# First product of a graph layer on one core: x in five pieces, and the row part of the first four steps on GpSimd

## The reference, cut to what matters

```python
h = maximum(layernorm(x), 0)
a = (adj + adj.T) * 0.5 + eye            # symmetrised, with self loops
deg = sum(a, axis=1)
d = where(deg > 0, deg ** -0.5, 0)
a = d[:, None] * a * d[None, :]
x = x + (adj @ a) @ h                    # first layer
h = maximum(layernorm(x), 0)
x = x + attention_and_dense(h, adj, ...) # second layer: 8 heads, then four dense layers
```

## Time and profile before

| | |
|---|---|
| median of 3 runs | 884.76 us (884.63 to 884.87) |
| profiled execution, time | 884.79 us |
| profiled execution, span | 882.9 us |
| TensorE busy | 855.8 us, 97% of the span |
| VectorE busy | 691.6 us, 78% |
| ScalarE busy | 414.5 us, 47% |
| GpSimd busy | 276.5 us, 31% |

### The profile page before, as it was taken

One profiled execution on the slowest core, in us unless ns is written; L12 is line 12 of the kernel. 1 busy time (PEld: TensorE's weight loads), 2 busy tenths in 40 slices (PEclk: granted clock), 3 DMA queues, 4 the chain that ended last, 5 costly groups with the idle time before them and its releaser, 6 DMA issues.

```text
span 882.9 us, 15244 instructions
## 1 busy us (share of the span) xinstructions
PE 855.8 (97%) x5145; PEld 751.5 (85%) x5145; DVE 691.6 (78%) x1188; ACT 414.5 (47%) x758; POOL 276.5 (31%) x293
## 2 busy tenths in 40 slices
PE   2999999999999999999799999999999999999998
PEld 1878888888888888878699999999999999999663
DVE  6789986556557775686999989999999999999722
ACT  3445433321111122345576666666666666775431
POOL 0000000000000000066738555555555655575222
PEclk9999999999999999999799999999999999999999
DMA  9959922603332321040160000000000032001033
GB/s 349 407 218 373 367 95 77 185 0 119 97 99 90 107 99 54 22 171 4 27 219 16 20 24 26 26 24 24 25 26 24 24 96 72 14 1 49 28 120 140
DMA packets 36117, 87.37 MB, mean 99 GB/s; under 512 B 7072, under 2 KB 7968, under 8 KB 36064
## 3 DMA queue, kind: packets, MB, share of 16 engines
q1 hardware_dynamic: 35024, 82.46, 26.7%
q0 software_dynamic: 1040, 4.26, 1.3%
HBM read 73.93 MB, written 12.78 MB: 98 GB/s over the span
## 4 chain that ended last, share of the span: by engine, by line
PE 90%; DVE 8%; DMA 1%; ACT 1%; issue 0%; ACTq 0%; DVEq 0%
PE bank L1578 25%; PE bank L73 15%; PE bank L75 15%; PE bank L74 15%; PE bank L1604 13%; DVE l_q L1227 3%; PE bank L2036 3%; PE bank L1998 1%; DVE e L859 1%; PE bank L2019 1%; PE bank L2028 1%; DMA l_h<-x 1%; DVE l_stats L784 1%; DVE x_lo L855 1%; PE bank L923 0%
## 5 line engine op out<-in xcount | busy, mean ns | idle before, releaser
L1227 DVE SCALAR_TENSOR_TENSOR l_q<-bank,neg_d,mask 128x512 fp32r<-128x512 f32 x512 | 338.7, 742 | 24.4 <-PE bank L1578 24.1
L1578 PE MATMUL bank<-l_parts,l_q 128*128 128x260 f32 x2048 | 252.0, 284 | 3.8 <-DVE l_q L1227 3.8
L1578 PEld LDWEIGHTS bank<-l_parts,l_q 128*128 128x128 f32 x2048 | 249.3, 190 | 4.3 <-issue 3.9
L73 PE MATMUL bank<-x_hi,s_hi 128*128 128x512 f32 x448 | 174.5, 389 | 0.0
L75 PE MATMUL bank<-x_hi,s_lo 128*128 128x512 f32 x448 | 174.3, 389 | 0.0
L74 PE MATMUL bank<-x_lo,s_hi 128*128 128x512 f32 x448 | 174.3, 389 | 0.0
L746 POOL TENSOR_TENSOR l_prod<-wh,l_a 128x512 f32<-128x512 f32 x30 | 36.3, 1229 | 389.0 <-ACT wh L718 389.0
L1351 ACT ACTIVATE l_mask<-mask 128x512 fp32r<-128x512 uint8 (+1 forms) x256 | 136.4, 619 | 0.1
L1604 PE MATMUL bank<-l_parts,l_mask 128*128 128x260 f32 x1024 | 128.8, 286 | 0.7 <-DVE l_parts L1233 0.7
L1604 PEld LDWEIGHTS bank<-l_parts,l_mask 128*128 128x128 f32 x1024 | 127.0, 189 | 1.0 <-ACT l_o_q L1357 0.9
L75 PEld LDWEIGHTS bank<-x_hi,s_lo 128*128 128x128 f32 x448 | 84.1, 188 | 17.6
(11 more groups left out here) (180 smaller groups left out, 1086.1 us busy)
## 6 DMA issues: line engine op xcount, KB each, us to landing
rows<-adj_t SPq DMA_DIRECT2D x48, 512.0 KB, 3.9
l_now<-adj SPq DMA_DIRECT2D x16, 512.0 KB, 7.5
l_rows_k<-adj_t SPq DMA_DIRECT2D x16, 512.0 KB, 8.3
l_src<-e_rows SPq DMA_DIRECT2D x30, 256.0 KB, 3.2
l_kept<-adj SPq DMA_DIRECT2D x12, 512.0 KB, 13.2
wh_store<-wh POOLq DMA_DIRECT2D x1, 4160.0 KB, 15.8
l_h<-x SPq DMA_DIRECT2D x4, 1024.0 KB, 17.4
x<-x SPq DMA_DIRECT2D x1, 4096.0 KB, 13.5
```

The source lines that it names most:

```text
L73: pe.matmul(acc, hi, rhs_hi, start=first, stop=False, skip_group_check=True)
L1227: v.scalar_tensor_tensor(out=q[:, i, :], in0=bank[S_BANKS[hh]][:], scalar=neg_d[:, i, h:h + 1], in1=mask[:, i, cols], op0=ALU.is_ge, op1=A ...
L1578: return pe.matmul(bank[Q_BANKS[hh][t]][:, 0:PW], q[:, i, t * P:(t + 1) * P], parts[pair_slot][:, hh, i, :], start=i == 0, stop=i == T - 1)
```

## The change

- x is loaded and normalised in five pieces instead of four: tile 0 alone, tiles 1 to 3, and then as before. The load of tile 0's row pieces stands between the first and the second piece.
- The lo part of the row half in steps 0 to 3 is made by GpSimd, in a loop of four subtractions, and counted on a semaphore of its own, early_lo_ready. TensorE in steps 0 to 3, and SyncE's loads of row tiles 4 to 7, wait for that count instead of lo_ready. VectorE adds 4 to lo_ready once.
- VectorE's list is written out for row tiles 0 and 1: the statistics of tile 1 stand between scale(0) and cut_x_lo(0), those of tiles 2 and 3 and the variances behind it; the six refine operations of tiles 1 to 3 are threaded between the small operations of row tile 1.
- ScalarE normalises tile 1 inside step 1 and tiles 2 and 3 one step ahead of their use; tile 0 alone comes first.
- Elsewhere, at the kernel's end, the semaphore last_stored is dropped; the last four stores are counted on the semaphore of their buffer.

```diff
-    CHUNKS = ((0, 4), (4, 8), (8, 12), (12, 16))
+    CHUNKS = ((0, 1), (1, 4), (4, 8), (8, 12), (12, 16))
...
-                sp.wait_ge(lo_ready, (before if before < EARLY else before + EARLY) + 1)
+                if before < EARLY:
+                    sp.wait_ge(early_lo_ready, before + 1)
+                else:
+                    sp.wait_ge(lo_ready, before + EARLY + 1)
...
         load_x(0)
-        for i in range(EARLY + 2):
+        load(0)
+        load_x(1)
+        for i in range(1, EARLY + 2):
             load(i)
-        load_x(1)
+        load_x(2)
...
-        for i in range(EARLY):
+        v.sem_inc(lo_ready, EARLY)
...
+        for i in range(2, EARLY):
             add_now(i)
             add_kept(i)
...
             scale(i)
-            cut_lo(i)
             cut_x_lo(i)
...
+            if i == 1:
+                normalise(1, 1, 2)
             cut_x_hi(i)
+            if i + 1 < EARLY:
+                normalise(1, i + 1, i + 2)
...
+        for s in range(EARLY):
+            p.wait_ge(hi_ready, s + 1)
+            p.tensor_tensor(s_lo[:, s % 2, :], step_source(s), s_hi[:, s % 2, :].bitcast(F32),
+                            ALU.subtract).then_inc(early_lo_ready, 1)
...
-            pe.wait_ge(lo_ready, s + 1)
+            if isinstance(s, int) and s < EARLY:
+                pe.wait_ge(early_lo_ready, s + 1)
+            else:
+                pe.wait_ge(lo_ready, s + 1)
...
-            done.then_inc(self.last_stored if step == 1 else self.stored[c % 2], 16)
+            done.then_inc(self.stored[c % 2], 16)
```

More of the change, by code:

```diff
@@ L153, in smooth_features @@
     lo_ready = sem("l0_lo_ready")
+    early_lo_ready = sem("l0_early_lo_ready")
     x_hi_ready = sem("l0_x_hi_ready")
@@ L202, in sync @@
         load_x(0)
-        for i in range(EARLY + 2):
+        load(0)
+        load_x(1)
+        for i in range(1, EARLY + 2):
             load(i)
-        load_x(1)
+        load_x(2)
         load(EARLY + 2)
         load(EARLY + 3)
-        load_x(2)
         load_x(3)
+        load_x(4)
         for i in range(FIRST_NOW, T):
@@ L219, in link, with statistics @@
             links[name] = len(links) + 1
-        def statistics(c):
+        def statistics(c, skip=0, stop=None):
             lo, hi = CHUNKS[c]
             v.wait_ge(x_loaded[c], 16)
-            for t in range(lo, hi):
+            for t in range(lo + skip, hi if stop is None else lo + stop):
                 v.bn_stats(stats[:, t - lo, :], h[:, t, :]).then_inc(ln_chain, 1)
@@ L309, in vector @@
             refine(0, n)
-        for i in range(EARLY):
+        v.sem_inc(lo_ready, EARLY)
+        add_now(0)
+        add_kept(0)
+        degree(0)
+        guard(0)
+        invert(0)
+        square(0)
+        correct(0)
+        scale(0)
+        statistics(1, 0, 1)
+        cut_x_lo(0)
+        statistics(1, 1)
+        variances(1)
+        add_now(1)
+        refine(1, 0)
+        add_kept(1)
+        refine(1, 1)
+        degree(1)
+        refine(1, 2)
+        guard(1)
+        refine(1, 3)
+        invert(1)
+        refine(1, 4)
+        square(1)
+        refine(1, 5)
+        correct(1)
+        scale(1)
+        cut_x_lo(1)
+        for i in range(2, EARLY):
             add_now(i)
@@ L324, in vector @@
         degree(4)
-        statistics(1)
+        statistics(2)
         guard(4)
-        variances(1)
+        variances(2)
         cut_lo(5)
@@ L330, in vector @@
         invert(4)
-        refine(1, 0)
+        refine(2, 0)
         add_kept(5)
         square(4)
-        refine(1, 1)
+        refine(2, 1)
         degree(5)
         correct(4)
-        refine(1, 2)
+        refine(2, 2)
         guard(5)
         scale(4)
-        refine(1, 3)
+        refine(2, 3)
         cut_lo(6)
-        refine(1, 4)
+        refine(2, 4)
         add_now(6)
-        refine(1, 5)
+        refine(2, 5)
         invert(5)
@@ L362, in vector @@
         cut_x_lo(8)
-        statistics(2)
+        statistics(3)
         invert(7)
-        variances(2)
+        variances(3)
         square(7)
@@ L370, in vector @@
         scale(7)
-        refine(2, 0)
-        statistics(3)
-        refine(2, 1)
+        refine(3, 0)
+        statistics(4)
+        refine(3, 1)
         cut_lo(10)
-        refine(2, 2)
+        refine(3, 2)
         cut_x_lo(10)
-        refine(2, 3)
-        variances(3)
-        refine(2, 4)
+        refine(3, 3)
+        variances(4)
+        refine(3, 4)
         add_now(8)
-        refine(3, 0)
-        refine(2, 5)
-        refine(3, 1)
+        refine(4, 0)
+        refine(3, 5)
+        refine(4, 1)
         add_kept(8)
-        refine(3, 2)
+        refine(4, 2)
         degree(8)
-        refine(3, 3)
+        refine(4, 3)
         guard(8)
-        refine(3, 4)
+        refine(4, 4)
         cut_lo(11)
-        refine(3, 5)
+        refine(4, 5)
         cut_x_lo(11)
@@ L472, in scalar @@
         cut_hi(0)
-        normalise(0, 1, 2)
         take_root(0)
-        normalise(0, 2, 3)
         cut_x_hi(0)
-        normalise(0, 3, 4)
+        take_ln_root(1)
         for i in range(1, EARLY):
@@ L485, in scalar @@
         take_root(4)
-        take_ln_root(1)
+        take_ln_root(2)
         cut_hi(5)
@@ L489, in scalar @@
         cut_hi(6)
-        normalise(1, 4, 6)
+        normalise(2, 4, 6)
         take_root(6)
         cut_hi(7)
-        normalise(1, 6, 8)
+        normalise(2, 6, 8)
         take_root(7)
@@ L498, in scalar @@
         cut_x_hi(9)
-        take_ln_root(2)
+        take_ln_root(3)
         cut_hi(10)
         cut_x_hi(10)
-        take_ln_root(3)
-        normalise(2, 8, 10)
+        take_ln_root(4)
+        normalise(3, 8, 10)
         cut_hi(11)
@@ L506, in scalar @@
         take_root(8)
-        normalise(2, 10, 12)
+        normalise(3, 10, 12)
         for i in range(9, T):
@@ L512, in scalar @@
             if i < 13:
-                normalise(3, i + 3, i + 4)
+                normalise(4, i + 3, i + 4)
         for s in range(FIRST_LATE - 1, STEPS):
@@ L1852, in __init__ @@
         self.stored = [sem(f"stored{b}") for b in range(2)]
-        self.last_stored = sem("last_stored")
     def load(self, sp, c, x1_store):
@@ L1868, in store @@
                 "(t p) f -> p t f", p=P), self.res[c % 2][:, t:t + step, :])
-            done.then_inc(self.last_stored if step == 1 else self.stored[c % 2], 16)
+            done.then_inc(self.stored[c % 2], 16)
     def wait_for_stores(self, sp):
-        for b in range(2):
-            sp.wait_ge(self.stored[b], 16 * ((self.NCH - b) // 2))
-        sp.wait_ge(self.last_stored, 16 * self.GT)
+        sp.wait_ge(self.stored[0], 16 * (self.NCH // 2))
+        sp.wait_ge(self.stored[1], 16 * (self.NCH // 2 - 1 + self.GT))
     def shares(self, v, c, count=1, fine=None, checked=None):
```

## The result

The changed kernel takes 889.21 us (median of 5 runs, 888.61 to 889.37) against 884.87 for the kernel before (5 runs, 884.63 to 885.00): ratio 1.0048, 95% interval 1.0033 to 1.0063, so 4.3 us slower. 889.0 was forecast. The profiled execution after took 889.21 us for a span of 887.4.

A forecast was written before the change was run, and what follows sets the result against it. TensorE is busy nine tenths or more nearly throughout, so its last early wait, before product 5, counts. Product 5 4.3 later, less 0.08 overlap twice, leaves +4.2: 884.79 + 4.2 = 889.0 us, range 884.6 to 890.6.

The forecast's parts named there:

- The mechanism: Early steps: a VectorE operation with two SBUF tensors, however small, makes no progress until the GpSimd operation under way ends.
- 768 KB less at 408 GB/s: Start: 768 KB no longer ahead of row tile 0, so its second half lands 1.93 us sooner, at 9.9.
- Rival (a): GpSimd's subtractions take 1.90 us: 0.5 less in each of three steps, 887.5; within the forecast's 0.52.
- Step 0: First row tile: add_kept(0) or square waits for GpSimd; first matmul at 16.2, the middle of 16.5 and 15.85.
- Step 1: Row tile 1: add_now(1) at 17.7, 128x3 refinement waits for GpSimd until 22.55; product 1 at 26.2, TensorE waits 1.9.
- Steps 2 and 3: Square waits for GpSimd until +4.85, so each step takes 7.05 us against a product's 5.62; product 3 at 40.2.
- The signs: Profile: first matmul 15.8 to 16.5, one-column operations over 1 us beside GpSimd, three TensorE waits together about 4.7 us.
- Rival (b): One-column tensor_scalars wait too, so everything from guard on comes 0.7 later in steps 2 and 3: 890.4; chance 0.15.
- Rival (c): One-column operations, square included, don't wait; only step 1 is late, product 5 +1.6: 886.4; chance 0.12.
- Rival (d): VectorE and GpSimd run side by side; product 5 still starts at 47.1 behind the x transfer: 884.8; chance 0.11.
- Rival (e): The clock falls in TensorE's new waits, priced at 2.5 us for one fall: 891.5; chance 0.06.
- Rival (f): Engines side by side and the queue quicker at the beginning, product 5 2.3 us sooner: 882.5; chance 0.04.

The follow-up runs named there:

- x1_first: x_only with the x of row tiles 1 to 3 moved ahead of the first row tile's loads again; 884.89 us, ratio 1.0005.
- pointers: Changed kernel with square and scale as tensor_scalar, their extra operands per-row scalars, so one SBUF tensor each; 887.76 us, ratio 1.0035 to the kernel before.
- x_only: Changed kernel with the four s_lo back on VectorE, x still in five pieces; 884.91 us, ratio 1.0001 to the kernel before.
- unlock: Changed kernel with pointers and kept_wait together, the refinement of tiles 1 to 3 ahead of add_now(1), and tile 1 normalised ahead of step 1; 884.79 us, ratio 1.0001.
- kept_wait: Changed kernel with GpSimd's first subtraction waiting until VectorE's add_kept(0) is done; 888.93 us, ratio 1.0050 to the kernel before.
- x_only_early: x_only with the x of row tiles 4 to 7 asked for one row tile earlier; 884.61 us, ratio 1.0000 to the kernel before.

## Why the prediction was right, step by step

The mechanism was right; it was named from two places 390 and 441 us into the trace and holds for the early steps. One of the three lines counted there, the 128x8 tensor_scalar of 0.94 us, has a single tensor and so is no case of two tensors; the other two (1.11 and 1.87) are. The total is close partly by luck, because misses cancelled: product 1 came 1.0 late, steps 2 and 3 gave 0.7 back, and between the end of the layer and the median 0.4 more went.

- **x and the first row tile.** x(0) was taken at 3.26 (3.95 forecast), now(0) at 8.52 (7.3), kept(0) at 11.12 (9.9). The term "768 KB less at 408 GB/s" was mis-sized: 0.7 us gained instead of 1.93. The full rate of the earlier trace rows was measured from 40 to 50 us; from 3 to 7 us the queue moves 215 to 229 GB/s. The seven kernels with this order all have that slow stretch (see x1_first); its cause stays open.
- **GpSimd's subtraction.** 2.34 to 2.40, forecast 2.40 from the earlier trace rows. Rival (a) falls.
- **Step 0.** Of the two orders allowed, GpSimd came first by 0.2 us, and add_kept(0) waited. For that order the working had 16.5; with GpSimd at 10.92 instead of 9.75 it gives 17.7, and 17.61 was measured. The middle of both orders, 16.2, is no time that either could give.
- **Product 0.** 7.3 us instead of 8.1 (see the last section). This changed nothing but TensorE's wait behind it, since VectorE's early_lo(1) sets when product 1 begins.
- **Step 1.** The refinement waited for GpSimd as forecast (21.60 to 23.81). add_now(1) began 1.3 late, at 18.99; product 1 came at 27.23, forecast 26.2, behind a wait of 2.33, forecast 1.9.
- **Steps 2 and 3.** 6.70 us instead of 7.05. Square waited as forecast. But the working let it start where GpSimd ends, and it ended there (31.79, GpSimd 31.77): from there to the end of early_lo it is 2.0, not 2.2. GpSimd ran from +2.39 to +4.77 of the step, not to +4.85, and the next step begins 0.08 ahead of early_lo's end. Two steps at 0.35 give back 0.7: product 3 at 40.65, forecast 40.2. Its wait was 0.41 us, and product 2 had none, since product 1 itself was slow.
- **The signs.** The first matmul is outside the 15.8 to 16.5 named. TensorE waits twice, 2.7 us in all, not three times and 4.7; most of the rest is in product 1, which was 1.8 us slower. A one-column operation waited beside two of GpSimd's four; beside the others it was add_kept(0) and the 128x3 product.
- **The sum.** The layer ends 391.23 - 386.50 = 4.7 us later, the span is 4.5 longer, the time 4.3; forecast 4.2. From product 5 on the shift is carried to the end, as said. The 0.4 between 4.7 and 4.3 was not traced; the medians of the kernel before differ by up to 0.2.
- **Rival (b), one-column tensor_scalars wait:** false. Guard inside GpSimd's stretch takes 0.15 us, twice. The Trainium skill, Advanced Engine Details and Errata, section "2x-2p Requirements", has the two-port mode only for an even dimension or an odd one above 1; the trace agrees for this one column, with no wait.
- **Rival (c), no operation of one column waits:** false; the squares took 1.51 and 1.53. pointers shows that an operation of the same size with one tensor doesn't wait. The Trainium skill, SBUF — State Buffer, section "Who interferes with whom", has a VectorE instruction with two SBUF inputs contend with a GpSimd instruction that reads SBUF, for ports that only one of them can hold; the runs agree down to 128x1, where 0.22 us of work took 1.41 to 1.74.
- **Rival (d), the gain hidden behind the x transfer:** false for the change, where the lock outweighs it, but it is what happens once the lock is away (x_only and unlock).
- **Rival (e), the clock:** it did fall, behind the wait of 2.33 us (0.58 from 27 to 31). Product 2 ended at 40.65 - 0.41 = 40.24, so it began at 34.6, and product 1 had taken 7.4 us instead of 5.62. But by this working it cost nothing: at 32.85 product 2 would have waited for VectorE until about 33.8, and product 3 would still have started at 40.65, since VectorE's chain decides there.
- **Rival (f), a quicker queue:** false; it was slower at the beginning, not quicker.

## What to carry to other kernels

Before a helper operation is given to GpSimd, list what VectorE has to run beside it: each operation with two SBUF tensors, even one of a single column, that began while GpSimd was at work on its SBUF tensors ended no sooner than GpSimd in these runs, so 0.2 us on the critical path became 1.5. Give VectorE work with one tensor (per-row scalars instead of a second tensor), or start GpSimd where VectorE's chain is waiting anyway. And follow the gain to the last wait: here a start 1.4 to 1.7 us earlier showed in no median, because a transfer that lands some 26 us later set when TensorE could go on.

## What was not expected of the hardware

**The first product runs at half pace until a moment that hardly follows its start.** TensorE after, around the change of pace:

```profile
20.30 0.62 PE L73 MATMUL bank<-l_early_hi,s_hi 128*128 128x512 f32 x1
20.73 0.43 PE L74 MATMUL bank<-l_early_lo,s_hi 128*128 128x512 f32 x1
21.00 0.39 PE L75 MATMUL bank<-l_early_hi,s_lo 128*128 128x512 f32 x1
21.23 0.39 PE L73 MATMUL bank<-l_early_hi,s_hi 128*128 128x512 f32 x1
21.46 0.39 PE L74 MATMUL bank<-l_early_lo,s_hi 128*128 128x512 f32 x1
```

Matmuls start 0.43 us apart until 20.7, and from 21.0 on 0.23. The change of pace lies near 21.4 before (start 16.62), 21.2 in x_only (15.21), 20.9 in unlock (14.92), 20.5 in kept_wait (16.64) and 22.6 in pointers (17.04). So product 0 took 8.5 us in x_only and 7.3 in after, and of the 2.4 us between their starts half is lost again; the other kernels lie between, with scatter. The granted clock reads 1.00 in all of this, though 0.43 us apart is also the pace from 28 to 30 us, where it reads 0.50. What sets the moment wasn't tested.

**The clock behind short waits.** Behind TensorE's waits of 2.33 and 2.04 us the granted clock fell to 0.50 for some 3 us; behind 1.34 us (pointers) and 0.94 us (x_only_early) it stayed at 1.00. One execution each.
